# Moving the causal maximum and the head addition behind the row numbers in VectorE's program

## The reference: what is computed

```python
# layer 1, for each of 8 heads
logits = leaky_relu(e_l[:, None] + e_r[None, :]) + gate * curv_bias     # 2048 x 2048
out    = softmax(where(adj > 0, logits, -1e9)) @ h
# layer 2, for each row and each of 8 heads
scores, idx = top_k(sim, 16)                  # two lists of 128 similarities
final, pk   = top_k(scores0 + scores1, 16)    # 16 of the pairs, and their row numbers
k = softmax(final) @ keys_table[rows];  v = softmax(final) @ values_table[rows]
sim  = where(causal, q @ k.T, -max)
attn = softmax(sim) @ v;  x = x + attn @ Wo
```

## Time and profile before

| | before |
|---|---|
| median of 3 runs | 4302.01 us (4301.11 to 4304.52) |
| the profiled execution | 4302.53 us, its span 4300.8 us |
| busy PE, DVE, ACT, POOL | 3427.1, 3315.0, 2259.3, 2047.6 us |
| mean granted TensorE clock | 0.919 |
| the interleaved stage | to about 3000 us, then the second graph attention and the experts |

### The profile page before, as it was taken

One profiled execution on the slowest core, in us unless ns is written; L12 is line 12 of the kernel. 1 busy time (PEld: TensorE's weight loads), 2 busy tenths in 40 slices (PEclk: granted clock), 3 DMA queues, 4 the chain that ended last, 5 costly groups with the idle time before them and its releaser, 6 DMA issues. The chain is left out here.

```text
span 4300.8 us, 61129 instructions
## 1 busy us (share of the span) xinstructions
PE 3427.1 (80%) x19161; PEld 2640.9 (61%) x19288; DVE 3315.0 (77%) x10546; ACT 2259.3 (53%) x3612; POOL 2047.6 (48%) x2052
## 2 busy tenths in 40 slices
PE   6867778777777788888888989665878888887799
PEld 4645555555555566666666666544667777776676
DVE  2679889898898898988988889774777777777434
ACT  5645455555555565565655656322555555555333
POOL 0377777777777777777767667661000000000000
PEclk9988889899999999999999999777899999999899
DMA  2244444455455555555556555553322122222200
GB/s 76 60 128 118 134 141 131 145 143 154 149 155 161 162 166 175 176 173 175 187 172 199 177 166 194 185 176 136 102 29 25 14 29 29 29 29 9 46 3 8
DMA packets 217422, 501.28 MB, mean 117 GB/s; under 512 B 63676, under 2 KB 115072, under 8 KB 210816
## 3 DMA queue, kind: packets, MB, share of 16 engines
q0 software_dynamic: 98304, 268.57, 21.4%
q1 hardware_dynamic: 118796, 228.80, 19.1%
HBM read 470.64 MB, written 26.41 MB: 116 GB/s over the span
## 5 line engine op out<-in xcount | busy, mean ns | idle before, releaser
L506 POOL DMA_INDIRECT ck_ring<-in_tables,ck_rows x2048 | 2047.4, 1000 | 884.0 <-issue 750.6
L991 DVE SCALAR_TENSOR_TENSOR ck_part<-ck_ring,ck_norm_w,ck_part 128x256 f32<-128x256 f32 x1792 | 770.0, 477 | 61.2 <-DVE ck_rows L966 41.7
L565 PE MATMUL psV<-ck_vals,ck_probsT 128*128 128x128 f32 x4096 | 556.5, 285 | 109.0 <-ACT ck_probsT L740 102.5
L550 PE MATMUL psL<-ck_bias_rhs,ck_bias_w 110*128 110x512 f32 x1024 | 573.4, 643 | 87.1 <-ACT ck_bias_rhs L727 38.5
L565 PEld LDWEIGHTS psV<-ck_vals,ck_probsT 128*128 128x128 f32 x4096 | 504.2, 197 | 157.8 <-ACT ck_probsT L740 89.0
L1253 PE MATMUL psL<-ga_probsT,ga_vals 128*128 128x256 f32 x2048 | 531.5, 407 | 0.7 <-ACT ga_probsT L1340 0.7
L740 ACT COPY ck_probsT<-psT 128x512 f32<-128x512 f32 x512 | 281.9, 587 | 446.4 <-PE psT L557 445.3
L1240 PE MATMUL psT<-ident,ga_probs 128*128 128x128 f32 x2048 | 300.2, 281 | 188.8 <-ACT ga_probsT L1340 187.6
L1253 PEld LDWEIGHTS psL<-ga_probsT,ga_vals 128*128 128x128 f32 x2048 | 399.5, 205 | 51.7 <-ACT ga_probsT L1340 0.9
L1240 PEld LDWEIGHTS psT<-ident,ga_probs 128*128 128x128 f32 x2048 | 248.3, 145 | 242.2 <-issue 214.5
L1331 ACT ACTIVATE ga_probs<-ga_probs,ga_neg_mx 128x2048 f32<-128x2048 f32 x128 | 256.4, 2003 | 225.4 <-DVE ga_neg_mx L1404 225.2
(11 more groups left out here) (210 smaller groups left out, 5455.7 us busy)
## 6 DMA issues: line engine op xcount, KB each, us to landing
ck_ring<-in_tables,ck_rows POOLq DMA_INDIRECT x2048, 2.8
ck_adj_raw<-in_adj SPq DMA_DIRECT2D x16, 1024.0 KB, 9.0
adj_scratch<-ck_adj_neg SPq DMA_DIRECT2D x16, 512.0 KB, 10.4
values_scratch<-ck_values_tile SPq DMA_DIRECT2D x128, 64.0 KB, 1.7
keysT_scratch<-ck_keys_tile SPq DMA_DIRECT2D x128, 64.0 KB, 1.9
ck_keysT<-keysT_scratch SPq DMA_DIRECT2D x8, 1024.0 KB
ck_values<-values_scratch SPq DMA_DIRECT2D x8, 1024.0 KB
ga_adj_neg<-adj_scratch SPq DMA_DIRECT2D x16, 512.0 KB, 11.6
```

The costliest lines, as they stand in the source:

```text
L506: pool.indirect_dma_start(ring[:, slot, :], None, ins["tables"], bass.IndirectOffsetOnAxis(rows[:, k, s:s + 1], axis=0)).then_inc(got[(u * ...
L550: last = nc.tensor.matmul(psL[:, c * CH:(c + 1) * CH], bias_w[:, :], bias_rhs[:, k % 2, c * CH:(c + 1) * CH], start=False, stop=True)
L565: last = nc.tensor.matmul(psV[:, k % 2, :], probsT[:, q % 2, s, :], vals[:, j, :], start=(j == 0), stop=(j == T - 1))
L991: done.append(c.did(nc.vector.scalar_tensor_tensor(part[:, s % 2, :], ring[:, slot, :], norm_w[:, s:s + 1], part[:, s % 2, :], ALU.mult, A ...
```

## The change

`attend_now()` goes from ahead of the compare to behind the two increments that follow the row numbers. The same instructions run, with the same operands and as many semaphores.

```diff
                     t4 = c.did(nc.vector.max_index(top_at[:, 8:16], top[:, 8:16], cand_rest[:, :]))
                     add_slots(1)
-                    attend_now()
                     dve.wait_ge(step, t4)
                     t5 = c.did(nc.vector.tensor_tensor(hit[:, :, :], ..., ALU.is_equal))
                     add_slots(1)
...
                     dve.wait_ge(step, found_rows)
                     dve.sem_inc(rows_ready, 1)
                     dve.sem_inc(sim_free, 1)
+                    attend_now()
                     if not adding_too:
                         c.restart()
```

## The result

| | before | after |
|---|---|---|
| median | 4301.56 us (4 runs, 4298.51 to 4304.52) | 4534.26 us (4 runs, 4532.87 to 4536.01) |
| ratio | | 1.0545, 95% interval 1.0528 to 1.0562 |
| span of the profiled execution | 4300.8 us | 4534.2 us |
| mean granted TensorE clock | 0.919 | 0.899 |

The move made the kernel 233 us slower. Forecast were 4515 us and a range of 4385 to 4575. The first rows are the page of the kernel after: busy time by engine, and then its granted clock in 40 slices (tenths of full speed).

A forecast was written before the change was run, and what follows sets the result against it. VectorE's own work was taken to bound a middle unit. Chain +129, tile ends 0, clock +119 and tail −35 gave +213 us on 4302.5, so 4515 us, range 4385 to 4575.

The forecast's parts named there:

- The added delay and who waits for it: Main loop: the maximum comes 4.09 us later, holding up `at_exp`, quarter 2's copy, `weigh`, projection, graph logits and next `max_of`.
- The chain against the cover: 86 middle main-loop units: the chain from `at_max` to the logits outlasts VectorE's own remaining work; 1.5 us each, +129 us.
- A rival that made the loss linear in the delay: From the expectation for run 3: loss proportional to the maximum's delay, 80 us for 1.4 us, giving 4380 us; no chance given.
- The clock: Middle units: the gap ahead of `weigh` of quarter 2 puts TensorE's low clock on the chain; +119 us, bounds 0 and 189.
- Tile ends: Last two units of each tile: what goes in ahead of `at_max` comes back behind it; 0, bounds −30 to +45 us.
- The tail: Last 8 units and entry: the compare to reduce stretch fills VectorE's wait for causal logits; −32 and −3, together −35 us.
- The faster one: Whole kernel: the tail gives 35 us and VectorE's slots cover the main-loop chain; 4267 us, chance 0.06.
- No change: Whole kernel: GpSimd's gathers set the pace and hide VectorE's order; about 4302 us, chance 0.04.
- Without the clock: Main loop: the longer chain costs time without the clock falling on it; 4396 us, or 4440 with up to 43, chance 0.27.
- The half-way case above the forecast: Half-way to the clock falling in all 86 middle units and tile ends costing too (4615 us): 4565 us; chance 0.13.

The follow-up runs named there:

- run 1: Kernel before, with only the addition of the finished head moved behind the row numbers and the causal maximum left ahead of the compare: 4303.94 us, ratio 1.0004.
- run 8: Changed kernel, with ScalarE's causal exponential moved behind all four copies of the turned quarters: 4269.34 us, ratio 0.9912 to the kernel before.
- run 5: Changed kernel, with extra products of a zero tile on TensorE in the gap ahead of `weigh` of quarter 2: 4338.61 us, ratio 1.0086 to the kernel before.
- run 3: Kernel before, with `attend_now()` moved behind the compare and one slot, about 1.4 us later, in main loop and tail: 4263.87 us, ratio 0.9912.
- run 2: Kernel before, with the move made only in the last 8 choices, the tail: 4270.33 us, ratio 0.9931.
- run 4: Kernel before, with `attend_now()` moved behind the multiply and two slots, 2.8 us later, in main loop and tail: 4294.57 us, ratio 0.9988.

## Why the prediction was right, step by step

- **The added delay and who waits for it.** Shown. The maximum comes about 4.1 us later, the addition doesn't matter (run 1), and the way to the loss leads through `at_exp` ahead of the copy of quarter 2: with that order changed the loss is gone (run 8).
- **The chain against the cover.** Its mechanism and size are shown by run 5, with the clock up: 9.76 us were worked out for the chain with 8 blocks and 1455.35 − 1445.60 = 9.75 measured, +129 us for the 86 units and +132.7 measured. The 11 units after the change whose chain kept the full clock grew by 1.5 each, the same figure without any extra products. The kink that goes with it was there: 1.4 us of delay cost the middle units 14 us, 2.8 cost 73, 4.1 cost 274. A rival that made the loss linear in the delay falls with run 3.
- **The clock.** The mechanism was right and its size too small. The term was +119 us in middle units, and 273.9 − 132.7 = 141.2 were measured. Two things were off. The 8-block chain grew by 12.58 − 9.79 = 2.8 us and not 2.2, and the low stretches reached further along the stage: middle units with 11 to 13 blocks grew by 3.0 to 3.5 us after the change, against 1.8 to 1.9 with the gap filled, and the sum had nothing for them. Together with the tile ends below, the clock cost about 197 us, not 119. Between the changed kernel and the one with the gap filled are 196 us, 4.3% of the time. The Trainium skill, "TensorE: Matmul & The Clock Gate", Part 1, puts the ramp's penalty under 1% of a typical kernel's span for modelling, by which my estimate was at most 43 us here. It says so of the ramp at the start of a run of products. The measurement decides: this kernel runs the chain at the low level in 75 of 86 middle units, and the page's figure doesn't carry over to it.
- **Tile ends.** Forecast 0, measured −2.7, and that is luck. With the clock up they gain 59 us, and the clock takes 56 back. So the sum left out a gain of 59 us and put the clock 78 us too low, and the two errors largely cancel. I had noted that part of the 5.35 us wait was TensorE at the low clock and set it against the rest without a number.
- **The tail.** −35 forecast, −36.5 measured, and run 2 has 31 of them alone.
- **Rivals.** The faster one is out: the middle units grew at every number of blocks, by 1.2 to 4.1 us. "No change" is out by the 233 us; and gathers that are released earlier, by 0.5 us in run 1 and by 1.6 us in the tail of run 2, cost nothing. "Without the clock" is out by run 5. The half-way case above the forecast, 4565, was too high, since its tile ends cost nothing net.

What stays open is when a gap brings the clock down. After gaps of 2.29 and 2.25 us it fell once and held once. Over all middle units the two cases overlap: on the chain it was low behind a gap of only 1.85 us (after, 14 blocks), and it stayed at 1.00 behind gaps of 3.55 us (after, 9 blocks) and 3.78 us (run 4, 2 blocks). The prediction would have been called wrong by a clock that stays at 1.00 where the gap is 3 to 5 us; of the 86 middle units after the change three had such a gap and kept the full clock on the chain. My expectations of runs 3 and 4 took every gap over 2 us for a fall on the path, and missed by 76 and 170 us.

## What to carry to other kernels

An instruction that costs its engine the same wherever it stands can cost 5% or gain 1.5% by where it stands, through what is queued behind its result on other engines. Before moving it, follow the result until it comes back to its own engine, and compare that time with the engine's own work in between: up to the difference a delay is nearly free, beyond it each unit pays the excess in full. Then place by stage: here the best place was behind the compare in most tiles (in the early ones ahead of it was as good or a little better), and last in the tail, where the engine waited anyway. And look at where TensorE's idle time goes, not only at its sum: a gap just ahead of products that others wait for can bring the low clock onto the path.

## What the runs showed of the hardware

Zero products put into a gap of TensorE raised the granted clock from 0.86 to 0.98 over 1260 us and took 196 us off the kernel, though TensorE then had more to do. I had expected about 140. The other surprise is the pair above: in two builds of the same loop with TensorE about as busy, gaps of equal length (2.29 and 2.25 us) were followed once by 16 products in 3.64 us and once in 2.05. Elsewhere the chain ran low behind a gap of 1.85 us and at the full clock behind one of 3.78, so the length of the gap just ahead doesn't sort the cases.
